# Closing stretch of a fused attention and expert-FFN kernel: gathered rows added before the last shared sum, a chained gather queue, and a re-cut last product

## The chip, the cores and the metric

One NeuronCore of a Trainium2 chip. The metric is the device time of one execution in microseconds; before the change the median of three runs is 760.45 (760.0 to 761.2).

## The reference, cut to what matters

```python
x = x + xattn(layernorm(x), ctx, ctx, Wq, Wk, Wv, Wfc, bfc)      # 8 x 256 tokens of 512 numbers
h = layernorm(x)                                                  # 2048 tokens in all
scores = softmax(h @ gate.T)                                      # 8 experts in 4 groups of 2
topk_w, topk_i = top 2 experts of the 2 best groups
routed = sum over the 2 experts of topk_w * ((silu(h @ gate_w.T) * (h @ up_w.T)) @ down_w.T)
shared = (silu(h @ sh_gate_w.T) * (h @ sh_up_w.T)) @ sh_down_w.T  # 704 wide: two halves of 352
x = x + routed + shared                                           # float32 out
```

## The kernel before, in words

Everything runs on one core. Attention takes the first 290 us, the output projection, second layernorm and routing run to about 390 us. The feed-forward part works in units: one unit is a tile of 128 tokens times one set of gate, up and down weights, and has a number w. `PA` = 16 units are the two halves of the shared expert on the first 8 token tiles ("early" tiles 0 to 7). `PB` = 36 units (slots) are the routed experts on tokens that were collected by expert; each writes its 128 result rows to `slot_y` in DRAM. `PC` = 16 units are the two halves of the shared expert on the last 8 token tiles ("late" tiles m = 0 to 7, token tile m + 8); their numbers run from `C0` to `TOTAL` - 1. The change is in this last part and a step ahead of it.

Weights and activations are cut in two float16 parts, so each product is made of three. A unit w goes like this. TensorE makes the gate product and then the up product (`gate_up`, L1510: 24 matmuls of 352 columns). ScalarE makes the silu (L1133). VectorE multiplies it with the up product (`hidden`, L2015); ScalarE squares and sums (L1138), VectorE turns the sum into a scale (L2020, L2023), ScalarE writes the scaled high part in float16 (L1143), VectorE the low part (`hidden_low`, L2028), which counts `h_cut`. SyncE then issues a DMA that transposes the hidden rows into `hT` (`h_rows`, L637). TensorE makes the down product from it (`down`, L1527: 9 matmuls of 512 columns) into bank 4 or 5. VectorE adds this product, scaled, to a row buffer (`add_down`, L2042), which counts `y_evac`. The scale comes from `down_factor` (L2036).

TensorE's order is up(w), down(w-2), up(w+1), down(w-1), and so on, so the down product of a unit comes two units after its up product. At the end there is no more up product: down(TOTAL-3), down(TOTAL-2), then six transposes on TensorE (L1690) in place of the DMA for the last unit, copies of both parts out of PSUM (high part ScalarE L1208, low part VectorE L2507), and the last down product (L1697).

The result of a token tile is x2 (the residual, loaded by SyncE into `res_out[q]`, L698) plus the shared sums plus two gathered rows of `slot_y`, each times a weight. `gather_1[q]` and `gather_2[q]` are filled by two indirect DMAs that GpSimd issues (L943); q = 2m is early tile m, q = 2m + 1 is late tile m. Every q has buffers of its own, and four semaphores (q % 4) count the gathers, four the residual loads. From q = 4 on GpSimd waits before the gathers of q until the output of q - 4 is finished (`out_done`). For a late tile VectorE adds the two shared products to `res_out` (`late_sum`), then, half a tile later, the two gathered rows (`late_out`, L2449 and L2452, the second one written to `gather_2[q]`). For an early tile, whose shared part is in x2 already, it only adds the gathered rows (`early_out`, L2428 and L2432). SyncE stores `gather_2[q]` (L702, the last tile L769). The last late tile adds its gathered rows first (L2512, L2514), and then both shared products.

All engines run an order written out by hand, and each engine issues strictly in that order. In the loop of VectorE (L2485) a round of m does unit (m, 0), then `late_out(m-2)` and `late_sum(m-1, 0)`, then unit (m, 1), an early output, and `late_sum(m-1, 1)`. On SyncE an `h_rows(w)`, a store that waits for its output, and loads follow each other in one queue.

`load_late` loads the transposed tokens of a late tile (L691). The first two of these loads are issued when SyncE comes to w = C0 - 2.

Of the kernel before, what the change touches and what calls it, by code (L numbers as in the profile page):

```python
# [30 lines left out]
P = 128  # L31
# [53 lines left out]
def build(nc, x, ctxT, wqT, wkvT, wfcT, bfc, gwT, wgu, wdn, out):  # L85
# [17 lines left out]
    with ExitStack() as ctx:  # L103
# [309 lines left out]
        TOTAL = PA + PB + PC  # L413
        LAST_PAR = (TOTAL - 1) % 2

        def early_done(m):
            return 2 * m if m < 3 else 2 * m - 1

        def late_done(m):
            return 2 * m + 1 if m < 2 else 2 * m + 2  # L420
# [9 lines left out]
        def _(sp):  # L430
# [269 lines left out]
            def store_out(t, done, q):  # L700
                sp.wait_ge(out_done, done + 1)
                sp.dma_start(tile_of(out_tiles, t), gather_2[q]).then_inc(out_st[q % 4], 16)  # L702
# [11 lines left out]
            for w in range(B0, C0):  # L714
# [19 lines left out]
                if m == SLOTS + 1:  # L734
                    for s in range(2):
                        sp.wait_ge(sx_ld[s], SX_SEEN + 16 * len(range(FIRST_ROWS + s, SLOTS, 2)))
                        load_late(s, s)

            def store_pair(m, side):
                store_out(m + side * EARLY, late_done(m) if side else early_done(m), 2 * m + side)  # L740

            for w in range(C0, TOTAL):
# [3 lines left out]
                if c == 0 and m >= 2:  # L746
                    store_pair(m - 2, 1)
                    if m < EARLY - 1:
                        load_pair(m, 1)
# [3 lines left out]
                if c == 1 and 1 <= m < EARLY - 1:  # L753
                    side_m = m - 1 if m < 3 else m
                    store_pair(side_m, 0)
                    load_pair(side_m + 2, 0)
                if c == 0 and m == EARLY - 1:
                    load_pair(m, 1)
                if c == 0 and m == 3:
                    store_pair(2, 0)  # L760
                    load_pair(4, 0)
# [4 lines left out]
            store_pair(EARLY - 1, 0)  # L766
            store_pair(EARLY - 2, 1)
# [7 lines left out]
        def _(pool):  # L775
# [160 lines left out]
            for q in range(2 * EARLY):  # L936
                t, m = q // 2 + q % 2 * EARLY, q // 2 - 2
                if q >= 4:
                    pool.wait_ge(out_done, (late_done(m) if q % 2 else early_done(m)) + 1)
# [272 lines left out]
        def _(pe):  # L1212
# [473 lines left out]
            late_down(TILES - EARLY - 1, 0)  # L1686
            pe.wait_ge(h_cut, TOTAL)
            for a in range(2):
                for j in range(NF):
                    tr = nc.tensor.transpose(last_hT[a][:, j, :], h16[LAST_PAR][:, a, j * P:(j + 1) * P], ident16)  # L1690
            tr.then_inc(xt_ready, 1)
            pe.wait_ge(h_high, TOTAL + 1)
            pe.wait_ge(h_cut, TOTAL + 1)
            pe.wait_ge(y_evac, TOTAL - 2)
            for j in range(NF):
                for n, (hp, wp) in enumerate(((0, 0), (0, 1), (1, 0))):
                    mm = nc.tensor.matmul(bank[Y_BANKS[LAST_PAR]][:], hT[LAST_PAR][:, hp, j, :], shared_dn(1)(wp, j),  # L1697
                                          start=(j == 0 and n == 0), stop=(j == NF - 1 and n == 2))
            mm.then_inc(dn_done, 1)
# [3 lines left out]
        def _(dve):  # L1703
# [718 lines left out]
            def early_out(m, half):  # L2422
# [4 lines left out]
                if half != 1:  # L2427
                    nc.vector.scalar_tensor_tensor(res_out[q], gather_1[q], w1[:, m:m + 1], res_out[q],  # L2428
                                                   ALU.mult, ALU.add).then_inc(step, 1)
                if half != 0:  # L2430
                    dve.wait_ge(step, links4 + early_done(m) + 1)
                    nc.vector.scalar_tensor_tensor(gather_2[q], gather_2[q], w2[:, m:m + 1], res_out[q],  # L2432
                                                   ALU.mult, ALU.add).then_inc(out_done, 1)

            def late_sum(m, c):
# [137 lines left out]
```

## Time and profile before

| what | value |
|---|---|
| median of 3 runs | 760.45 us |
| the profiled execution | 761.22 us |
| its span in the profile | 759.3 us |
| TensorE busy (matmul) | 734.4 us, 97% of the span |
| VectorE / ScalarE / GpSimd busy | 561.4 / 418.1 / 265.1 us |
| granted TensorE clock, mean | 0.993 of full |

The span is one execution as the hardware profiler saw it; the execution's own time has 1.9 us around it. "Busy" of TensorE counts each matmul from its issue to its modelled end, and they overlap. A row of a timeline gives the start in us, the duration, the engine, the line of the kernel, the operation and its tiles. In brackets stands how long the engine was idle before and what ended that. SPq is SyncE's queue: its rows are issues of DMAs, not the transfers.

### The profile page before, as it was taken

What the parts mean: (1) busy time and instruction counts of PE and PEld (TensorE: products, weight loads), DVE (VectorE), ACT (ScalarE), POOL (GpSimd) and SP (SyncE); (2) the same over time, 40 slices, a digit from 0 to 9 for tenths busy, and PEclk for the clock granted to TensorE, in tenths of its full rate; (3) what the DMA queues carried; (4) which work ended last, traced back from release to release, by engine and by line L of the source; (5) the groups of instructions that cost most, each with busy time, mean ns of one, the idle gap of its engine ahead of it and who ended that gap; (6) DMA issues with size and microseconds to landing.
All of it is one profiled execution on the core that took longest, in us unless ns stands there. A gap on an engine that the chain in (4) does not pass through costs nothing.

```text
span 759.3 us, 16085 instructions
## 1 busy us (share of the span) xinstructions
PE 734.4 (97%) x5316; PEld 398.3 (52%) x5317; DVE 561.4 (74%) x1191; ACT 418.1 (55%) x845; POOL 265.1 (35%) x219
## 2 busy tenths in 40 slices
PE   6999999999999999999999899999999999999997
PEld 4554534443344335666655456555555556655553
DVE  5677779999999967897589787555555555447767
ACT  3567568888888884777632554343434334232232
POOL 3254007999996302556200021111111110015431
PEclk9999989999999999999999999999999999999999
DMA  8998846565664798997586564977777789549995
GB/s 326 353 413 259 252 151 207 180 197 165 201 182 131 238 370 324 358 398 239 170 230 195 147 155 123 190 180 180 183 170 184 172 180 206 139 116 297 278 263 158
DMA packets 155099, 168.15 MB, mean 221 GB/s; under 512 B 97952, under 2 KB 111776, under 8 KB 154528
## 3 DMA queue, kind: packets, MB, share of 16 engines
q1 hardware_dynamic: 143724, 126.20, 57.1%
q0 software_dynamic: 10720, 40.12, 17.4%
q10 hardware_dynamic: 596, 1.07, 0.4%
q8 instruction: 35, 0.57, 0.3%
q14 instruction: 24, 0.20, 0.1%
HBM read 104.09 MB, written 41.42 MB: 192 GB/s over the span
## 4 chain that ended last, share of the span: by engine, by line
PE 78%; DVE 10%; ACT 4%; DMA 4%; issue 3%; SPq 1%; DVEq 0%; ACTq 0%
PE psum L1510 24%; PE psum L1527 13%; PE psum L1356 9%; PE psum L1342 6%; PE psum L1437 6%; PE psum L1270 4%; PE psum L1512 3%; PE psum L1246 3%; PE psum L1373 2%; PE psum L1529 2%; PE psum L1455 1%; PE psum L1222 1%; DMA x_dram<-sb_rows 1%; DVE sb_stats L1742 1%; ACT sb_weights L1064 1%
## 5 line engine op out<-in xcount | busy, mean ns | idle before, releaser
L1510 PE MATMUL psum<-sb_weights,sb_rows 128*128 128x352 f16 (+1 forms) x1344 | 209.7, 313 | 0.9 <-DVE sb_h L2028 0.6
L1510 PEld LDWEIGHTS psum<-sb_weights,sb_rows 128*128 128x128 f16 x1344 | 131.2, 98 | 77.7 <-issue 1.9
L1761 DVE TENSOR_REDUCE sb_rows<-psum 128x4 f32<-128x1024 f32 x128 | 149.9, 1214 | 4.5 <-PE psum L1270 4.5
L1064 ACT ACTIVATE sb_weights<-psum 128x512 f32<-128x512 f32 x256 | 139.4, 595 | 23.1 <-PE psum L1342 19.9
L1527 PE MATMUL psum<-sb_weights,sb_hT 128*128 128x512 f16 (+1 forms) x531 | 125.4, 382 | 0.0
L923 POOL DMA_INDIRECT sb_rows<-xn_rows,sb_slot_tok x36 | 35.5, 986 | 209.3 <-DVE sb_rows L2394 134.6
L1138 ACT ACTIVATE psum<-psum 128x352 f32<-128x352 f32 x68 | 30.5, 448 | 118.4 <-DVE psum L2015 118.3
L1342 PE MATMUL psum<-sb_weights 50*128 50x512 f16 x256 | 87.2, 390 | 1.7 <-ACT sb_weights L1064 0.9
L1356 PE MATMUL psum<-sb_weights 128*32 128x256 f32 x1024 | 83.1, 397 | 0.3
L1527 PEld LDWEIGHTS psum<-sb_weights,sb_hT 128*128 128x128 f16 x531 | 51.9, 98 | 56.0 <-issue 2.2
L1270 PE MATMUL psum<-sb_weights 48*128 48x256 f16 x512 | 71.3, 275 | 0.6 <-DVE sb_rows L1761 0.4
L943 POOL DMA_INDIRECT sb_weights<-slot_y,sb_p_i x32 | 31.7, 990 | 81.2 <-DMA slot_y<-sb_rows 42.6
L1437 PE MATMUL psum<-sb_weights 128*128 128x512 f32 x128 | 58.2, 597 | 0.3 <-ACT sb_weights L1070 0.3
L2028 DVE SCALAR_TENSOR_TENSOR sb_h<-psum,sb_h_scale_i,sb_h 128x352 f16<-128x352 f32 x68 | 39.6, 583 | 22.5 <-ACT sb_h L1143 22.4
L2015 DVE SCALAR_TENSOR_TENSOR psum<-psum,sb_inv_now,sb_h 128x352 f32<-128x352 f32 x36 | 21.3, 593 | 45.6 <-PE psum L1510 33.6
L1342 PEld LDWEIGHTS psum<-sb_weights 50*128 50x128 f16 x256 | 23.5, 93 | 55.1 <-ACT sb_weights L1064 45.9
L1133 ACT ACTIVATE sb_h<-psum,sb_inv_now 128x352 f32<-128x352 f32 x36 | 19.9, 553 | 50.6 <-PE psum L1510 38.5
L1246 PE MATMUL psum<-sb_weights 128*128 128x512 f16 x192 | 44.9, 380 | 2.5 <-DVE sb_weights L1811 1.3
L1143 ACT ACTIVATE sb_h<-psum,sb_h_scale_i 128x352 f16<-128x352 f32 x68 | 37.6, 553 | 17.2 <-DVE sb_h_scale_i L2020 17.2
L829 POOL TENSOR_TENSOR sb_weights<-sb_weights,sb_w_scale_i 128x1408 f32<-128x1408 f32 x15 | 38.0, 2531 | 23.3 <-ACT sb_weights L1110 22.5
L839 POOL TENSOR_TENSOR sb_weights<-sb_weights 128x1408 f16<-128x1408 f32 x15 | 43.0, 2863 | 1.2
L1133 ACT ACTIVATE sb_h<-psum,sb_w_inv_i 128x352 f32<-128x352 f32 x32 | 17.7, 554 | 45.8 <-PE psum L1510 44.9
(304 smaller groups left out, 1161.0 us busy)
## 6 DMA issues: line engine op xcount, KB each, us to landing
sb_weights<-in_wgu SPq DMA_DIRECT2D x20, 704.0 KB, 7.1
sb_weights<-in_wgu POOLq DMA_DIRECT2D x20, 704.0 KB, 6.0
sb_weights<-in_wdn SPq DMA_DIRECT2D x17, 768.0 KB, 5.7
slot_y<-sb_rows SPq DMA_DIRECT2D x36, 256.0 KB, 2.3
sb_weights<-q_parts SPq DMA_DIRECT2D x96, 64.0 KB, 2.9
x_dram<-sb_rows SPq DMA_DIRECT2D x24, 256.0 KB, 4.4
q_parts<-sb_weights SPq DMA_DIRECT2D x16, 256.0 KB, 4.1
sb_rows<-in_x POOLq DMA_DIRECT2D x16, 256.0 KB, 5.2
```

Of the source, the lines that this page charges most:

```text
L829: nc.gpsimd.tensor_tensor(stage, stage, scale.broadcast_to([P, HALF]), ALU.mult).then_inc(gu_scaled, 1)
L839: nc.gpsimd.tensor_tensor(low, stage, high, ALU.subtract).then_inc(gu_cut, 1)
L1064: nc.scalar.activation(probs[G % 2][:, kt, pair * 512:(pair + 1) * 512], bank[4 + f % 2], ACT.Exp, scale=exp_by[n]).then_inc(exp_done, 1)
L1246: mm = nc.tensor.matmul(bank[Q_BANKS[n][m]], wq16[:, wp, k, m * P:(m + 1) * P], xnT[n % 2][:, xp, k, :], start=(k == 0 and i == 0), stop=( ...
L1270: mm = nc.tensor.matmul(bank[banks[qt] + side][:, h * SEQ:(h + 1) * SEQ], q_st[s][lo:hi, g, h, b * SEQ + qt * P:b * SEQ + (qt + 1) * P], k ...
L1342: nc.tensor.matmul(bank[4 + side].rearrange("p (h t) -> p h t", h=HH), k_st[s][lo:hi, g, b * SEQ + kt * P:b * SEQ + (kt + 1) * P], q_st[s] ...
L1356: mm = nc.tensor.matmul(bank[6][VW * c:VW * (c + 1), 0:SEQ], v_now, probs[G % 2][:, kt, c * SEQ:(c + 1) * SEQ], start=(kt == 0), stop=(kt ...
L1437: mm = nc.tensor.matmul(bank[2 + s][:], oT[s][:, k, :], wfc_sb[:, k, :], start=(k == 0), stop=(k == KD - 1))
L1510: mm = nc.tensor.matmul(to[:, 0:F], x_T[:, at:at + P], gu(wp, k, which), start=first, stop=last)
L1527: mm = nc.tensor.matmul(bank[Y_BANKS[par]][:], hT[par][:, hp, j, :], dn(wp, j), start=first, stop=last)
L1761: nc.vector.tensor_reduce(to[:, :, j // UB, :, j % UB, qt], psum[:, banks[qt] * 512:(banks[qt] + 2) * 512] .rearrange("p (a h k) -> p a h ...
L2028: nc.vector.scalar_tensor_tensor(h16[par][:, 1, 0:F], bank[GU_BANKS[par][1]][:, 0:F], h_scale[:, par:par + 1], h16[par][:, 0, 0:F], ALU.mu ...
```

## The change

Parts, in the order of the diff:

- The first two `load_late` are issued at w = C0 - 3 instead of C0 - 2 (`m == SLOTS`), behind the same wait for the transposes of the routed slots' rows.
- The early outputs have other places: `EARLY_AT` says after which unit of the late part each is added and stored, the last two (6 and 7) both in unit (6, 0).
- Late tiles 0 and 1 are as before. From m = 2 on the gathered rows are added between the two shared sums (`late_gathered`, in unit (m+1, 1)), and the second shared sum goes to `gather_2[q]` and finishes the output. Late tile 6 and 7 have an order of their own at the end. SyncE stores these late tiles by `y_evac` instead of `out_done`.
- GpSimd's gathers of q >= 4 wait for the gathers of q - 4 to land, no longer for an output.
- On TensorE the six last transposes stand after the fifth of the nine matmuls of down(TOTAL-2). The last down product is made in two halves of 256 columns, into banks 0 and 1, 18 matmuls in all, with a count after each half; VectorE adds it in two halves as well.

```diff
         TOTAL = PA + PB + PC
+        last_y = [bank[b] for b in GU_BANKS[TOTAL % 2]]
         LAST_PAR = (TOTAL - 1) % 2
 
+        SUM_FIRST = 2
+        EARLY_AT = {(1, 1): (0,), (2, 1): (1,), (3, 0): (2,), (4, 0): (3, 4), (5, 0): (5,), (6, 0): (6, 7)}
+
         def early_done(m):
-            return 2 * m if m < 3 else 2 * m - 1
+            return min(2 * m, m + SUM_FIRST)
 
         def late_done(m):
-            return 2 * m + 1 if m < 2 else 2 * m + 2
+            return 2 * m + 1
+
+        def late_summed(m):
+            return C0 + 2 * m + 2
 
         def shared_inv(c):
...
-                if m == SLOTS + 1:
+                if m == SLOTS:
                     for s in range(2):
                         sp.wait_ge(sx_ld[s], SX_SEEN + 16 * len(range(FIRST_ROWS + s, SLOTS, 2)))
                         load_late(s, s)
...
-            def store_pair(m, side):
-                store_out(m + side * EARLY, late_done(m) if side else early_done(m), 2 * m + side)
+            def store_early(m):
+                sp.wait_ge(out_done, early_done(m) + 1)
+                store_out(m, 2 * m)
+
+            def store_late(m):
+                if m < SUM_FIRST:
+                    sp.wait_ge(out_done, late_done(m) + 1)
+                else:
+                    sp.wait_ge(y_evac, late_summed(m))
+                store_out(m + EARLY, 2 * m + 1)
...
-                if c == 0 and m >= 2:
-                    store_pair(m - 2, 1)
-                    if m < EARLY - 1:
-                        load_pair(m, 1)
+                if c == 0 and 2 <= m < 2 + SUM_FIRST:
+                    store_late(m - 2)
+                    load_pair(m, 1)
...
-                if c == 1 and 1 <= m < EARLY - 1:
-                    side_m = m - 1 if m < 3 else m
-                    store_pair(side_m, 0)
-                    load_pair(side_m + 2, 0)
-                if c == 0 and m == EARLY - 1:
-                    load_pair(m, 1)
-                if c == 0 and m == 3:
-                    store_pair(2, 0)
-                    load_pair(4, 0)
+                for e in EARLY_AT.get((m, c), ()):
+                    store_early(e)
+                    load_pair(e + 2, 0)
+                if c == 1 and SUM_FIRST < m < EARLY - 1:
+                    store_late(m - 1)
+                    load_pair(m + 1, 1)
...
-            store_pair(EARLY - 1, 0)
-            store_pair(EARLY - 2, 1)
+            store_late(EARLY - 2)
...
-                t, m = q // 2 + q % 2 * EARLY, q // 2 - 2
+                t = q // 2 + q % 2 * EARLY
                 if q >= 4:
-                    pool.wait_ge(out_done, (late_done(m) if q % 2 else early_done(m)) + 1)
+                    pool.wait_ge(gat_ld[q % 4], q // 4 * 32)
...
-            late_down(TILES - EARLY - 1, 0)
-            pe.wait_ge(h_cut, TOTAL)
-            for a in range(2):
-                for j in range(NF):
-                    tr = nc.tensor.transpose(last_hT[a][:, j, :], h16[LAST_PAR][:, a, j * P:(j + 1) * P], ident16)
-            tr.then_inc(xt_ready, 1)
+            def last_transposes():
+                pe.wait_ge(h_cut, TOTAL)
+                for a in range(2):
+                    for j in range(NF):
+                        tr = nc.tensor.transpose(last_hT[a][:, j, :], h16[LAST_PAR][:, a, j * P:(j + 1) * P], ident16)
+                tr.then_inc(xt_ready, 1)
+
+            m, par = TILES - EARLY - 1, (TOTAL - 2) % 2
+            pe.wait_ge(hT_ld[par], (m + C0 // 2) * 16 + 16)
+            pe.wait_ge(y_evac, TOTAL - 3)
+            for j in range(NF):
+                for n, (hp, wp) in enumerate(((0, 0), (0, 1), (1, 0))):
+                    mm = nc.tensor.matmul(bank[Y_BANKS[par]][:], hT[par][:, hp, j, :], shared_dn(0)(wp, j),
+                                          start=(j == 0 and n == 0), stop=(j == NF - 1 and n == 2))
+                    if (j, n) == (1, 1):
+                        last_transposes()
+            mm.then_inc(dn_done, 1)
             pe.wait_ge(h_high, TOTAL + 1)
             pe.wait_ge(h_cut, TOTAL + 1)
-            pe.wait_ge(y_evac, TOTAL - 2)
-            for j in range(NF):
-                for n, (hp, wp) in enumerate(((0, 0), (0, 1), (1, 0))):
-                    mm = nc.tensor.matmul(bank[Y_BANKS[LAST_PAR]][:], hT[LAST_PAR][:, hp, j, :], shared_dn(1)(wp, j),
-                                          start=(j == 0 and n == 0), stop=(j == NF - 1 and n == 2))
-            mm.then_inc(dn_done, 1)
+            for half in range(2):
+                here = slice(half * D // 2, (half + 1) * D // 2)
+                for j in range(NF):
+                    for n, (hp, wp) in enumerate(((0, 0), (0, 1), (1, 0))):
+                        mm = nc.tensor.matmul(last_y[half][:, 0:D // 2], hT[LAST_PAR][:, hp, j, :], shared_dn(1)(wp, j)[:, here],
+                                              start=(j == 0 and n == 0), stop=(j == NF - 1 and n == 2))
+                mm.then_inc(dn_done, 1)
...
+            def late_sum(m, c, to=None):
 
                 q, n = 2 * m + 1, m // 2
                 if c == 0:
                     dve.wait_ge(cx2_ld[q % 4], n * 16 + (16 + CX2_SEEN))
                 else:
                     dve.wait_ge(y_evac, m * 2 + (C0 + 1))
-                add_down(m * 2 + (C0 + c), (C0 + c) % 2, (C0 + c) % 2, res_out[q])
+                if to is not None:
+                    dve.wait_ge(step, steps[0])
+                add_down(m * 2 + (C0 + c), (C0 + c) % 2, (C0 + c) % 2, res_out[q] if to is None else to)
+
+            def late_gathered(m, half, summed):
+
+                q, n, t = 2 * m + 1, m // 2, m + EARLY
+                if half != 1:
+                    if summed:
+                        dve.wait_ge(y_evac, m * 2 + (C0 + 1))
+                    dve.wait_ge(cx2_ld[q % 4], n * 16 + (16 + CX2_SEEN))
+                    dve.wait_ge(gat_ld[q % 4], n * 32 + 32)
+                    nc.vector.scalar_tensor_tensor(res_out[q], gather_1[q], w1[:, t:t + 1], res_out[q],
+                                                   ALU.mult, ALU.add).then_inc(step, 1)
+                    steps[0] += 1
+                if half != 0:
+                    dve.wait_ge(step, steps[0])
+                    nc.vector.scalar_tensor_tensor(gather_2[q], gather_2[q], w2[:, t:t + 1], res_out[q],
+                                                   ALU.mult, ALU.add).then_inc(step, 1)
+                    steps[0] += 1
...
-            for m in range(2, EARLY):
+            for m in range(2, last):
                 late_unit(m, 0)
                 late_low(m, 0)
-                late_out(m - 2)
+                if m < 2 + SUM_FIRST:
+                    late_out(m - 2)
                 late_sum(m - 1, 0)
                 late_factor(m, 0)
-                if m == 3:
-                    early_out(2, None)
-                if m == last:
-                    early_out(last, 0)
-                    hidden(m * 2 + (C0 + 1), (C0 + 1) % 2, shared_inv(1))
-                    early_out(last, 1)
-                    hidden_factor(m * 2 + (C0 + 1), (C0 + 1) % 2)
-                    late_low(m, 1)
+                for e in EARLY_AT.get((m, 0), ()):
+                    early_out(e)
+                late_unit(m, 1)
+                late_low(m, 1)
+                if m > SUM_FIRST:
+                    late_gathered(m - 1, None, True)
+                    late_sum(m - 1, 1, gather_2[2 * m - 1])
                 else:
-                    late_unit(m, 1)
-                    late_low(m, 1)
-                    early_out(m - 1 if m < 3 else m, None)
-                late_sum(m - 1, 1)
+                    for e in EARLY_AT.get((m, 1), ()):
+                        early_out(e)
+                    late_sum(m - 1, 1)
                 late_factor(m, 1)
-            late_out(last - 1)
+            m, to, q = last, gather_2[2 * last - 1], TILES - 1
+            late_unit(m, 0)
+            late_low(m, 0)
+            late_gathered(m - 1, None, False)
+            late_sum(m - 1, 0, to)
+            late_factor(m, 0)
+            hidden(m * 2 + (C0 + 1), (C0 + 1) % 2, shared_inv(1))
+            late_gathered(m, 0, False)
+            hidden_factor(m * 2 + (C0 + 1), (C0 + 1) % 2)
+            late_low(m, 1)
+            late_sum(m - 1, 1, to)
             dve.wait_ge(xt_ready, SLOTS + 1)
             nc.vector.tensor_copy(hT[LAST_PAR][:, 1, :, :], last_hT[1]).then_inc(h_cut, 1)
-            m, q = last, TILES - 1
-            dve.wait_ge(cx2_ld[q % 4], m // 2 * 16 + (16 + CX2_SEEN))
-            dve.wait_ge(gat_ld[q % 4], m // 2 * 32 + 32)
-            link = chain(links4 + late_done(m - 1) + 1)
-            link(nc.vector.scalar_tensor_tensor(res_out[q], gather_1[q], w1[:, TILES - 1:TILES], res_out[q],
-                                                ALU.mult, ALU.add))
-            link(nc.vector.scalar_tensor_tensor(gather_2[q], gather_2[q], w2[:, TILES - 1:TILES], res_out[q],
-                                                ALU.mult, ALU.add))
-            for c in range(2):
-                if c == 1:
-                    dve.wait_ge(y_evac, TOTAL - 1)
-                add_down(TOTAL - 2 + c, (C0 + c) % 2, (C0 + c) % 2, gather_2[q])
+            late_factor(m, 1)
+            late_gathered(m, 1, False)
+            late_sum(m, 0, gather_2[q])
+            par = (C0 + 1) % 2
+            dve.wait_ge(y_evac, TOTAL - 1)
+            dve.wait_ge(y_factor, TOTAL)
+            for half in range(2):
+                here = slice(half * D // 2, (half + 1) * D // 2)
+                dve.wait_ge(dn_done, TOTAL + half)
+                done = nc.vector.scalar_tensor_tensor(gather_2[q][:, here], last_y[half][:, 0:D // 2], y_scale[:, par:par + 1],
+                                                      gather_2[q][:, here], ALU.mult, ALU.add)
+            done.then_inc(y_evac, 1)
```

## Rows read from the trace of the kernel before

**Rows 1.** The page: busy time, and the group of the gathers.

```profile
PE 734.4 (97%) x5316; PEld 398.3 (52%) x5317; DVE 561.4 (74%) x1191; ACT 418.1 (55%) x845; POOL 265.1 (35%) x219
...
L943 POOL DMA_INDIRECT sb_weights<-slot_y,sb_p_i x32 | 31.7, 990 | 81.2 <-DMA slot_y<-sb_rows 42.6
```

**Rows 2.** Waits, 655 to 760 us: who waited for whom, total, times, longest.

```profile
PE psum L1697 <- ACT sb_hT L1208: 1.6, 1, 1.6
...
PE psum L1510 <- DMA sb_rows<-xnT_dram: 0.3, 1, 0.3
```

**Rows 3.** Timeline of TensorE where the first two late units begin.

```profile
660.27 0.38 PE L1531 MATMUL psum<-sb_weights,sb_hT 128*64 128x512 f16 x1
660.96 3.75 PE L1510 MATMUL psum<-sb_weights,sb_rows 128*128 128x352 f16 x24 [0.31 <-DMA sb_rows<-xnT_dram]
...
666.40 0.38 PE L1531 MATMUL psum<-sb_weights,sb_hT 128*64 128x512 f16 x1
666.71 3.75 PE L1510 MATMUL psum<-sb_weights,sb_rows 128*128 128x352 f16 x24
```

**Rows 4.** Timeline of SyncE's queue ahead of that.

```profile
647.75 2.09 SPq L708 DMA_TRANSPOSE sb_rows<-sb_rows  x1
...
658.26 0.92 SPq L691 DMA_DIRECT2D sb_rows<-xnT_dram  x2
```

**Rows 5.** Timeline of VectorE: units (3,0), (3,1), (4,0) and a factor.

```profile
698.34 0.59 DVE L2015 SCALAR_TENSOR_TENSOR psum<-psum,sb_w_inv_i,sb_h 128x352 f32<-128x352 f32 x1 [0.52 <-PE psum L1510]
...
704.71 0.59 DVE L2015 SCALAR_TENSOR_TENSOR psum<-psum,sb_w_inv_i,sb_h 128x352 f32<-128x352 f32 x1
...
709.62 0.58 DVE L2015 SCALAR_TENSOR_TENSOR psum<-psum,sb_w_inv_i,sb_h 128x352 f32<-128x352 f32 x1
...
714.40 0.21 DVE L2036 TENSOR_SCALAR sb_stats<-sb_h_root,sb_dn_inv_i 128x1 f32<-128x1 f32 x1
```

**Rows 6.** Chain that ended last, 733 to 757 us: start, length, what.

```profile
733.38 3.58 PE psum L1510 x24
736.96 1.94 PE psum L1527 x9
...
756.00 0.75 DVE sb_weights L2042
```

**Rows 7.** Timeline of all engines, 744 us to the end.

```profile
744.26 3.74 PE L1510 MATMUL psum<-sb_weights,sb_rows 128*128 128x352 f16 x24
...
747.78 0.75 DVE L2428 SCALAR_TENSOR_TENSOR sb_weights<-sb_weights,sb_w 128x512 f32<-128x512 f32 x1 [0.25 <-issue]
747.84 4.05 PE L1527 MATMUL psum<-sb_weights,sb_hT 128*128 128x512 f16 x18
...
748.45 0.58 DVE L2015 SCALAR_TENSOR_TENSOR psum<-psum,sb_w_inv_i,sb_h 128x352 f32<-128x352 f32 x1
...
750.42 0.58 DVE L2028 SCALAR_TENSOR_TENSOR sb_h<-psum,sb_h_scale_i,sb_h 128x352 f16<-128x352 f32 x1 [0.42 <-ACT sb_h L1143]
...
751.73 0.50 PE L1690 MATMUL psum<-sb_tri,sb_h 128*128 128x128 f16 x6
...
752.32 0.48 ACT L1208 COPY sb_hT<-psum 128x384 f16<-128x384 f16 x1 [1.93 <-PE psum L1690]
...
753.35 0.35 DVE L2507 COPY sb_hT<-psum 128x384 f16<-128x384 f16 x1
...
753.80 2.10 PE L1697 MATMUL psum<-sb_weights,sb_hT 128*128 128x512 f16 x9 [1.58 <-ACT sb_hT L1208]
...
756.78 0.33 SPq L769 DMA_DIRECT2D out<-sb_weights  x1
```

**Rows 8.** Transposing DMAs of the hidden rows, 680 to 760 us: issue to landing.

```profile
DMA to landing us min/median/max: 2.7/3.9/6.6
```

**Rows 9.** Stretches: length; busy PE, PEld, DVE, ACT, POOL; clock; DMA share; GB/s.

```profile
680.00:700.00 20.00, 20.00 (x120) 11.58 (x119) 12.26 (x27) 6.33 (x16) 13.02 (x14) 1.00 0.99 271
700.00:720.00 20.00, 20.00 (x124) 11.91 (x122) 15.45 (x31) 5.83 (x14) 7.92 (x8) 1.00 1.00 305
```

More of the change, by code:

```diff
@@ L698, in load_res, with store_out @@
                 sp.dma_start(res_out[q], tile_of(x2_dram, t)).then_inc(cx2_ld[q % 4], 16)
-            def store_out(t, done, q):
-                sp.wait_ge(out_done, done + 1)
+            def store_out(t, q):
                 sp.dma_start(tile_of(out_tiles, t), gather_2[q]).then_inc(out_st[q % 4], 16)
@@ L2419, in _, with early_out @@
                 slot_factor(m, m % 2)
-            def early_out(m, half):
+            def early_out(m):
                 q, n = 2 * m, m // 2
@@ L2426, in early_out @@
                 dve.wait_ge(gat_ld[q % 4], n * 32 + 32)
[L2427 to L2435, printed above, removed]
+                nc.vector.scalar_tensor_tensor(res_out[q], gather_1[q], w1[:, m:m + 1], res_out[q],
+                                               ALU.mult, ALU.add).then_inc(step, 1)
+                steps[0] += 1
+                dve.wait_ge(step, steps[0])
+                nc.vector.scalar_tensor_tensor(gather_2[q], gather_2[q], w2[:, m:m + 1], res_out[q],
+                                               ALU.mult, ALU.add).then_inc(out_done, 1)
+            def late_sum(m, c, to=None):
                 q, n = 2 * m + 1, m // 2
@@ L2441, in late_sum @@
                     dve.wait_ge(y_evac, m * 2 + (C0 + 1))
-                add_down(m * 2 + (C0 + c), (C0 + c) % 2, (C0 + c) % 2, res_out[q])
+                if to is not None:
[12 more added lines that the diff above has]
+                if half != 0:
+                    dve.wait_ge(step, steps[0])
+                    nc.vector.scalar_tensor_tensor(gather_2[q], gather_2[q], w2[:, t:t + 1], res_out[q],
+                                                   ALU.mult, ALU.add).then_inc(step, 1)
+                    steps[0] += 1
             def late_out(m):
@@ L2450, in late_out @@
                                                ALU.mult, ALU.add).then_inc(step, 1)
-                dve.wait_ge(step, links4 + late_done(m) + 1)
+                steps[0] += 1
+                dve.wait_ge(step, steps[0])
                 nc.vector.scalar_tensor_tensor(gather_2[q], gather_2[q], w2[:, t:t + 1], res_out[q],
@@ L2480, in _ @@
             late_low(1, 1)
-            early_out(0, None)
+            early_out(0)
             late_sum(0, 1)
```

2 lines of the change are left out of this document (1 added, 1 removed).

## The prediction

> **What bounds the kernel now.** I read the page's busy times first: TensorE is busy 97% of the span, the next engine, VectorE, 74% [rows 1]. So the question is when TensorE is *not* running in the stretch that is changed, and that is what the table of waits answers: between 655 and 760 us TensorE waited twice, 0.3 us for a load at the start of the late part and 1.6 us for the copy of the transposed rows before the very last product [rows 2]. In between it works through a fixed grid: an up product of 3.58 us (24 matmuls) and a down product of 1.94 us (9 matmuls), 5.52 us per unit [rows 6]. Nothing that VectorE, GpSimd or SyncE do faster between 662 and 748 us can move that grid. Only three places can: the load's wait, the chain from the last up product to the last down product, and what follows the last down product. I then read the timeline around each [rows 3, 4, 7].
>
> **Part 1, the first late loads one step earlier.** The last down matmul of a slot starts at 660.27 and the up product at 660.96, 0.69 later; the same change-over six us later takes 0.31 (666.40 to 666.71) [rows 3]. The difference, about 0.37 us, is the wait. The loads were issued at 658.26 [rows 4]. One step earlier in SyncE's order they come behind the last transposing DMA of the slots, issued at 647.75 and 2.09 long, whose landing they wait for. Transposes of hidden rows land 2.7 to 6.6 us after issue [rows 8], so I take 650.5 to 654.4 for it; two issues take 0.92, so the loads are out by 655.3 at the latest, 3 us sooner than now and 5 us before they are needed. What is moved past in SyncE's queue is the `h_rows` of the next unit, which comes one 5.52 us unit after the one before it and is not due until then. Gain 0.37; bounds 0 (the load still lands last) and 0.37.
>
> **Part 2, the order of outputs and sums, and the chained gathers.** The number of 512-column VectorE operations stays the same. What is new: in units (4,0) and (6,0) VectorE has a sum and four output operations in a row, and a second shared sum waits for the gathered add just ahead of it. Such a full unit stands in the trace: from the start of unit (3,0)'s `hidden` to that of (3,1) 6.37 us pass (698.34 to 704.71), 0.85 over the grid; from (3,1) to (4,0), with two output operations and a sum, 4.91 us (to 709.62), so 0.61 is made up per unit [rows 5]. From (6,0) the backlog is 0.85 at (6,1). With 0.12 for the lost overlap of the dependent sum (an estimate: 0.08 by which VectorE's operations overlap, 748.53 against 748.45 [rows 7], and a semaphore of 0.03 to 0.04 as in 756.75 to 756.78 [rows 6, 7]) it is 0.36 at (7,0) and below zero at (7,1). Cost 0, hidden by the grid; were the cover gone, 0.36 us would reach the end. A late `hidden` does not touch TensorE before: `h_cut` of unit w is 2.55 us after its `hidden` (1.97 + 0.58 [rows 7]), and the up product that needs it starts 7.46 us after the last one ended.
>
> The gathers: from first to last they now spread over 31.7 us of issue and 81.2 - 42.6 = 38.6 us of idle [rows 1]. Without the wait for outputs some part of the 38.6 goes, so the last ones land up to 38 us earlier, long before the outputs that use them. Nobody in the waits stood still for a gather [rows 2], so this gains 0. Its cost is traffic: from 680 to 700 us, with 13 us of gather issue, the DMA engines are 0.99 busy, from 700 to 720 us already 1.00 with only 8 [rows 9]. The slack that pays for it: a transpose issued 2.6 us after its up product is needed 11.04 us after it, so 8.4 us from issue, and the longest took 6.6 [rows 8]. Cost 0; bounds 0 and the rival below.
>
> **Part 3, the closing chain.** The last up product ends at 748.00 (744.26 + 3.74), but `hidden` starts at 748.45, because an early output sits ahead of it (747.78 + 0.75 = 748.53) [rows 7]. After the change that place is empty: the gathered add of the last tile stands behind `hidden`. So `hidden` starts at 748.04, 0.41 earlier, and `hidden_low`, 1.97 later, runs from 750.01 to 750.59.
>
> The 18 down matmuls from 747.84 are 0.216 apart [rows 6, 7]; the second product begins at 749.78 and its fifth matmul's place ends at 750.86. That is where the transposes now start (the rows are ready at 750.59 plus 0.1), against 751.73. ScalarE's copy begins 0.59 after the transposes begin (752.32) and takes 0.48: 751.45 to 751.93. VectorE's copy, 0.35, waited for by two output operations before (753.35), now has only a 0.75 sum ahead of it, done at 751.3: 751.45 to 751.80. TensorE follows a copy by 0.10 (753.70 to 753.80) [rows 7], which gives 752.03; its own queue has six transposes (0.33 to 0.50) and four matmuls (0.86) from 750.86, so 752.05 to 752.22. I take 752.1 for the start of the last product, against 753.80: 1.7 us.
>
> The halves: 3.58 / 24 = 0.149 us for 352 columns and 1.94 / 9 = 0.216 for 512 make 0.415 ns per column and 0.109 for 256 [rows 6]. 18 of them take 1.97 us, as 9 whole ones did. The last one ends 0.16 after its place (2.10 - 1.94 [rows 6, 7]): 754.23. A VectorE operation of this kind takes 0.58 for 352 and 0.75 for 512 columns, so 0.48 for 256. VectorE itself is ready for the second half at about 754.1: copy to 751.80, factor 0.21 [rows 5], gathered add 0.75, sum 0.75, first half 0.48 and some 0.04 between each. So the end of the last add is 754.27 + 0.48 = 754.75, against 756.00 + 0.75 = 756.75 [rows 6]. The store and its landing stay as they are. Gain 2.00. Bounds: 1.6 if TensorE starts at 752.22 and the halves save nothing (754.35 + 0.04 + 0.75 = 755.14), 2.2 if the copies and the transposes overlap a little more.
>
> Two rules of the Trainium skill are weighed against this part. "TensorE: Matmul & The Clock Gate", Back-to-back issue gap, gives 262 cycles for 256 columns and 518 for 512, and a separate sustained figure of 131 ns for 512. The trace has 216 ns for 512, so by the trace the cycle figures hold here and the sustained one doesn't; by them two halves cost 6 cycles more than a whole product, 0.02 us over nine pairs. "VectorE: DVE Perf Modes", the section on the TRN2 errata, says an operation pays a fixed cost and that tiles should have 512 elements or more, which speaks against the two half adds. The rows agree that there is one, about 0.2 us. It is paid twice, but the first time lies under the second half of the product. The page's figure for a PSUM source (120 cycles and one per element at 0.96 GHz, 0.39 us for 256) would make the sum 0.09 larger.
>
> **Sum.** 0.37 + 0 + 2.00 = 2.37 us. Against the profiled execution's 761.22 that is 758.85; the profiled one is 0.77 above the median, so on the median of 760.45 it is 758.1. Its own range is 757.4 to 758.8.
>
> **Rivals.**
> 1. *The transpose of unit TOTAL-2 lands late.* This one has no 8.4 us: with the 0.36 of backlog it is issued at about 745.5 and needed at 749.7, 4.2 us later. It landed in 2.7 with nothing beside it; now a store and a load go out just ahead of it, about 742.7. Against: gathers no longer run there. At 5.9 us the stall is 1.7: 759.8; at the longest landing, 6.6, it is 2.4 and the gain is gone: 760.5.
> 2. *VectorE sets the end.* If the backlog of the double outputs isn't made up and `hidden` comes 0.85 late instead of on time, all of part 3 moves by it: 758.1 + 0.85 = 758.95. For: VectorE has only 0.1 to spare before the second half. Against: the 0.61 per unit.
> 3. *The first loads do not come sooner in effect* (the change does not do what it says): 0.37 less, 758.5. For: they wait for transposes in a busy stretch.
> 4. *Slower: the dense gathers hold up the transposes between 690 and 720 us.* Eight more gathers of 256 KB in the 20 us from 700 add 105 GB/s to 305, where the engines are full [rows 9]. From a landing of 8.4 us down products wait. A stall delays the next three units together, so six units make two stalls; slower than before from 9.6 us, and at 10.4 us it is 2 x 2.0 - 2.37 = +1.6: 762.1. Against: 6.6 was the longest with 13 gathers in a stretch, and the gathers limit themselves by waiting for those of q - 4.
>
> **Chances.** Forecast 0.60, rival 1 0.12, rival 2 0.12, rival 3 0.08, rival 4 0.06, others 0.02. A measurement of this kernel can tell about 0.2%, 1.5 us, from no change; faster means under 758.9. The forecast gives 0.56 of that, rival 2 half of its share, rival 3 most: 0.69. Slower is rival 4: 0.06. The range 757.4 to 760.2 leaves out rival 4, the worse end of rival 1 and a little below.
>
> **What would show it.** TensorE's waits: no load at 660 us and none of 1.6 us before the last product. The last up product ends at about 747.6 and `hidden` follows within 0.1. Transposes begin 2.9 us after that end, the last product 4.1, the final store 6.8 (now 8.8). If a wait for `hT` stands before down(TOTAL-2), rival 1; waits before down products around 700 to 720 us, rival 4; `hidden` over 0.3 behind the last up product, rival 2. The prediction is wrong in kind if the up product ends later than 748.0.

## The result, and the profile after

The changed kernel took 782.66 us (median of 4, 782.05 to 785.86), the kernel before beside it 760.83 (760.0 to 764.17): a ratio of 1.0287, 95% interval 1.0245 to 1.0329. It is slower by 22 us, where 758.1 was forecast, outside the range. The profiled execution has a span of 780.4 us against 759.3.

The first view is again the page: busy times, the clock row, and the group of the gathers.

```profile
PE 740.1 (95%) x5325; PEld 399.2 (51%) x5326; DVE 561.5 (72%) x1192; ACT 418.4 (54%) x845; POOL 264.8 (34%) x219
...
PEclk9999999999999999999999999999999999995899
...
L952 POOL DMA_INDIRECT sb_weights<-slot_y,sb_p_i x32 | 31.3, 979 | 53.2 <-DMA slot_y<-sb_rows 42.0
```

Beside [rows 1] the idle time of the gathers went from 81.2 to 53.2 us, as meant, and the clock row has one slice at 5, about 702 to 722 us, and one at 8 after it. That slice is where to look. The stretches of the changed kernel (length; busy PE, PEld, DVE, ACT, POOL; granted clock; DMA share; GB/s):

```profile
680.00:700.00 20.00, 20.00 (x122) 11.75 (x120) 11.66 (x26) 4.98 (x12) 13.93 (x15) 1.00 0.95 256
700.00:720.00 20.00, 8.14 (x28) 2.54 (x26) 2.87 (x6) 1.66 (x4) 15.12 (x17) 0.63 0.84 265
720.00:740.00 20.00, 16.40 (x78) 8.01 (x78) 11.42 (x24) 3.88 (x9) 1.80 (x2) 0.77 0.62 178
740.00:760.00 20.00, 20.00 (x124) 11.93 (x122) 14.94 (x33) 6.64 (x16) 0.00 (x0) 1.00 0.68 184
```

Against [rows 9], 700 to 720 us has 28 matmuls instead of 124, and VectorE and ScalarE do as little; only GpSimd works on, 17 gathers instead of 8. Over these 20 us the DMA engines are *less* busy than before, 0.84 instead of 1.00 (full only at the start, 1.09 from 700 to 704 us). The whole loss lies here: 96 matmuls missing in this stretch and 42 in the next (78 instead of 120) are 23 us of a grid that has 33 in 5.52 us. The mean granted clock of the stretch is 0.63, so most of it runs at the lower level, 1.2 GHz. The clock is still at 1.00 from 700 to 704 us, where TensorE has begun to idle, so it fell after the idling and did not cause it. It is at 1.00 again from 730 us.

What ended TensorE's idle time stands in its timeline (start, length, what, and in brackets the idle time before it):

```profile
698.81 2.11 PE L1536 MATMUL psum<-sb_weights,sb_hT 128*128 128x512 f16 x9
700.75 0.76 PE L1519 MATMUL psum<-sb_weights,sb_rows 128*128 128x352 f16 x4
701.90 0.46 PE L1519 MATMUL psum<-sb_weights,sb_rows 128*128 128x352 f16 x2 [0.38 <-issue]
702.61 0.31 PE L1519 MATMUL psum<-sb_weights,sb_rows 128*128 128x352 f16 x1 [0.25 <-issue]
703.32 0.61 PE L1519 MATMUL psum<-sb_weights,sb_rows 128*128 128x352 f16 x3 [0.40 <-issue]
705.44 0.74 PE L1519 MATMUL psum<-sb_weights,sb_rows 128*128 128x352 f16 x2 [1.52 <-issue]
...
724.39 4.15 PE L1536 MATMUL psum<-sb_weights,sb_hT 128*128 128x512 f16 x8 [0.82 <-issue]
```

The rows from 700.75 to 705.44 are *inside* one up product, whose 24 matmuls wait for nothing between them. "issue" is idle time for which the trace shows no wait. The starts 701.90, 702.61, 703.32 are 0.71 apart, and 705.44 three times that: instructions reach TensorE one or a few at a time. The last row shows what the clock adds: eight down matmuls take 4.15 us at the lower level (0.50 from 724 to 728 us), where nine take 2.11 at the upper. The other engines, from the product before to the end of the stall:

```profile
695.23 3.74 PE L1519 MATMUL psum<-sb_weights,sb_rows 128*128 128x352 f16 x24
...
704.14 0.55 ACT L1142 ACTIVATE sb_h<-psum,sb_w_inv_i 128x352 f32<-128x352 f32 x1 [8.05 <-remote]
...
716.02 0.59 DVE L2036 SCALAR_TENSOR_TENSOR psum<-psum,sb_w_inv_i,sb_h 128x352 f32<-128x352 f32 x1 [16.89 <-remote]
...
718.01 0.58 DVE L2049 SCALAR_TENSOR_TENSOR sb_h<-psum,sb_h_scale_i,sb_h 128x352 f16<-128x352 f32 x1 [0.42 <-issue]
...
721.16 0.95 POOL L952 DMA_INDIRECT sb_weights<-slot_y,sb_p_i  x1 [0.30 <-issue]
...
725.89 1.21 SPq L644 DMA_TRANSPOSE sb_hT<-sb_h  x1
```

The up product ended at 698.97, and ScalarE's silu of it starts 5.2 us later. VectorE's `hidden` needs that silu, done at 704.69, and starts 11.3 us later. SyncE's queue needs the rows that VectorE has finished at 718.59, and issues their transpose 7.3 us later. What runs has its usual length (0.55, 0.59). So these are not engines waiting for each other: four instruction streams hardly move, though what they need is there, while GpSimd issues a gather each 1.25 us. They do not recover together. VectorE and ScalarE run a whole chain in their usual rhythm from 716.02 to 720.03 us, with gathers still going out; TensorE and SyncE's queue come back after the last gather, issued at 721.16.

The rest of the prediction can be read beside it. No load is waited for at 660 us, and the end of the changed kernel is this:

```profile
767.35 3.74 PE L1519 MATMUL psum<-sb_weights,sb_rows 128*128 128x352 f16 x24
...
771.41 0.58 DVE L2036 SCALAR_TENSOR_TENSOR psum<-psum,sb_w_inv_i,sb_h 128x352 f32<-128x352 f32 x1
...
774.03 0.51 PE L1699 MATMUL psum<-sb_tri,sb_h 128*128 128x128 f16 x6
...
775.24 2.13 PE L1718 MATMUL psum<-sb_weights,sb_hT 128*128 128x256 f16 x18
...
776.59 0.48 DVE L2566 SCALAR_TENSOR_TENSOR sb_weights<-psum,sb_stats,sb_weights 128x256 f32<-128x256 f32 x1
777.41 0.48 DVE L2566 SCALAR_TENSOR_TENSOR sb_weights<-psum,sb_stats,sb_weights 128x256 f32<-128x256 f32 x1 [0.33 <-PE psum L1718]
777.92 0.33 SPq L778 DMA_DIRECT2D out<-sb_weights  x1
```

From the end of the last up product (771.09) the transposes begin 2.94 us later, the last product 4.15, the store 6.83; it was 8.78 [rows 7].

### The profile page after: what moved, and what is told of

It reads as the page before. It is cut to its first block, busy times and chain, and to the rows that moved or that the text cites. A ratio compares the mean times of both kernels' runs of the same rounds, so it can differ in the third digit from the quotient of the medians.

```text
span 780.4 us, 16110 instructions
## 1 busy us (share of the span) xinstructions
PE 740.1 (95%) x5325; PEld 399.2 (51%) x5326; DVE 561.5 (72%) x1192; ACT 418.4 (54%) x845; POOL 264.8 (34%) x219
## 4 chain that ended last, share of the span: by engine, by line
PE 79%; DVE 7%; DMA 6%; issue 4%; ACT 3%; SPq 2%; DVEq 0%; ACTq 0%
PE psum L1519 24%; PE psum L1536 13%; PE psum L1365 7%; PE psum L1446 7%; PE psum L1351 5%; PE psum L1521 4%; PE psum L1255 4%; PE psum L1279 3%; DMA sb_weights<-k_parts 3%; PE psum L1538 2%; PE psum L1382 2%; PE psum L1231 2%; DMA sb_weights<-in_x 1%; PE psum L1464 1%; PE psum L1236 1%
## 5 line engine op out<-in xcount | busy, mean ns | idle before, releaser
L1519 PE MATMUL psum<-sb_weights,sb_rows 128*128 128x352 f16 (+1 forms) x1344 | 214.1, 314 | 13.3 <-issue 12.8
L952 POOL DMA_INDIRECT sb_weights<-slot_y,sb_p_i x32 | 31.3, 979 | 53.2 <-DMA slot_y<-sb_rows 42.0
```

The source lines that it names most:

```text
L1519: mm = nc.tensor.matmul(to[:, 0:F], x_T[:, at:at + P], gu(wp, k, which), start=first, stop=last)
```

## The experiments

The theory after the result: gathers that follow each other without a gap keep the other engines from issuing. In all experiments but the first every transposing transfer is a plain copy of the same bytes; "plain" means that below. Each group that ran together shares its runs of the kernel before; ratios are to these, and between groups only ratios are compared.

**A small program.** Are such gathers enough by themselves? Each stage gives every engine a fixed load and GpSimd one of eight tasks.

```
for q in range(pairs):                       # 16 pairs of 2 gathers
    if q >= back: pool.wait_ge(gat[(q - back) % 4], done[q - back])
```

> A small program of its own that leaves the whole computation out and writes zeros. In each of eight stages TensorE has 192 matmuls 128x512 f16 (41 us at 0.216), ScalarE 64 copies 128x512, VectorE 48 sums 128x512 and SP's queue 12 loads of 0.26 MB (36 in the last two), while GpSimd has in turn: nothing; 16 pairs of gathers, each waiting for the pair four earlier to land; the same with a 0.95 us fill after each pair; 32 plain loads in place of the gathers; two pairs under way instead of four; only 6 pairs; nothing beside 36 loads; 16 pairs beside 36 loads. Theory (gathers without a gap starve the issue of the other engines by themselves): stages 2, 5 and 8 are 15 to 25 us longer than stage 1, stages 3 and 6 within 3 us of it. Rival M (the stall needs what else is queued in the kernel, loads, stores and transposes): stage 2 within 2 us of stage 1, and only stage 8 longer, if any. Rival D (it is the depth under way): stage 5 as stage 1. Rival G (it is the indirect addressing): stage 4 as stage 1; if it is the software queue as such, stage 4 as stage 2.

It took 406.5 us. Its stretches, first in the stage without gathers, then with 16 pairs, then with 16 pairs beside 36 loads:

```profile
30.00:40.00 10.00, 10.00 (x48) 4.51 (x46) 10.00 (x17) 10.00 (x20) 0.00 (x0) 1.00 0.39 107
...
80.00:90.00 10.00, 10.00 (x49) 4.52 (x47) 9.20 (x15) 10.00 (x21) 7.56 (x9) 1.00 0.93 312
...
370.00:380.00 10.00, 10.00 (x48) 4.51 (x46) 10.00 (x17) 10.00 (x20) 7.56 (x9) 1.00 1.04 387
```

TensorE has 48 matmuls in 10 us in all of them, also beside gathers in the rhythm of the stall (7.56 us of GpSimd in 10, as there) with the DMA engines at 1.04. The stages with 16 pairs came out longer only because the gathers themselves run on after the other work (in stage 3, with the fills, to 164.13 us, where TensorE has finished at 149.17). The first form of the theory, gathers by themselves, did not hold on this chip. The program has no loops, though, and TensorE and ScalarE run loops in the late part of the kernel.

**The plain kernels.** Does the stall need the transposing transfers?

```
-                sp.dma_start(hT[s]..., h_sb[s]..., transpose=True)
+                sp.dma_start(hT[s]..., h_sb[s]...)
```

> The kernel before with every transposing transfer (of the hidden rows and of the gathered slot rows) as a plain copy of the same bytes; so the rows stand untransposed in the down products, and this part of the computation is changed, here and in the runs called plain. It is the base for them. The copies should land sooner than the 2.7 to 6.6 us of the transposes, the order of the work stays: 752 to 762 us, no stall between 700 and 725 us.

> The changed kernel with plain copies. Theory L (the gathers without a gap starve the other engines where these run loops and much else is queued, whatever it is): the stall of 700.9 to 725 us is there again, 19 to 24 us over the plain before. Theory T (the stall needs transposing transfers in the same stretch, since the small program had none and no stall): no stall, 1.5 to 2.5 us under the plain before.

Plain before: 759.5 us (10 runs, 756.8 to 761.6), ratio to the kernel before 0.9970 (0.9955 to 0.9986). Plain changed: 782.15 (4 runs, 781.5 to 782.9), ratio 1.0268 (1.0250 to 1.0286). The stall is there without a single transposing transfer; rival T fell. One expectation was missed on the way: the copies do not land sooner, 4.7 us in the middle (2.1 to 5.6, in q1 below) against 3.9 for the transposes (2.7 to 6.6).

**Parts put back or taken alone.** These four ran together, on a second chip, without the plain changed kernel beside them. So a run without a stall says little here until it is known that the chip shows one.

> The changed kernel with plain copies, and one thing put back: each of the 12 late pairs of gathers waits again until the output four pairs earlier is summed. Theory L (gathers without a gap, in this kernel): the stall goes, what the first loads (0.38) and the closing chain (1.95) gave stays: 756.5 to 758 us against 759.5 of the plain before. Rival A (the new order of outputs and sums on VectorE and of stores and loads in SP's queue made the stall): within 3 us of the 782.2 of the plain changed kernel.

> The kernel before with plain copies and one thing of the change: the late pairs of gathers wait only for the pair four earlier to have landed. Theory L: the whole loss by itself, 759.5 + 19 to 24 us = 779 to 784 us. Rival A (orders): 759 to 761 us.

> The plain changed kernel with one fill 128x1024 on GpSimd (0.97 us) after each of the 12 late pairs; the waits stay those of the change. If pace decides, the stall is gone or under 8 us: 757 to 765 us. If it needs only that gathers are never waited for: still over 775 us.

> The plain changed kernel with each of the 32 gathers as an ordinary load of 128 rows of the same table through the same software queue, same bytes and same waits (the summed rows are then others). If the stall comes of the indirect addressing: gone, 757 to 759 us. If of many transfers of the software queue under way: still there, 770 to 783 us. GpSimd issues such a load in 0.55 us instead of 0.98, so the rate is higher.

The edits: in o3 the gathers wait for `out_done` and `y_evac` of four pairs earlier; o4 is the plain before with `pool.wait_ge(gat_ld[q % 4], q // 4 * 32)` alone; o5 is the plain changed kernel with

```
+                if q >= 4:
+                    pool.wait_ge(pause, q - 4)
+                    nc.gpsimd.memset(rows[:, 4 * D:6 * D], 0.0).then_inc(pause, 1)
```

and o6 has `nc.gpsimd.dma_start(to, slot_y_tiles[2 * q + n])` for each gather. None stalled:

| run | us, median (range), runs | ratio, 95% interval |
|---|---|---|
| o3 old waits | 761.6 (757.8 to 764.8), 10 | 1.0023 (1.0001 to 1.0044) |
| o4 before, chained | 758.7 (757.4 to 760.6), 10 | 0.9974 (0.9951 to 0.9996) |
| o5 fill after each pair | 755.4 (754.4 to 758.2), 7 | 0.9939 (0.9911 to 0.9968) |
| o6 plain loads | 758.5 (756.0 to 764.3), 10 | 0.9966 (0.9938 to 0.9993) |

o4 is a miss for the theory: the same chained gathers in the kernel before, and no loss. o3 went half as expected, no stall but none of the gain. Its waits say why (engine, line, releaser: total, times, longest):

```profile
DVE sb_weights L2455 <- DMA sb_weights<-slot_y,sb_p_i: 3.8, 1, 3.8
...
PE psum L1714 <- DVE sb_weights L2070: 1.8, 1, 1.8
PE psum L1706 <- DVE sb_h L2056: 1.5, 1, 1.5
```

VectorE stands 3.8 us for a gather and hands the delay on to TensorE at the end. The new order of outputs takes its rows earlier, so it *needs* gathers that run ahead of the outputs; it can't be had with the old pacing. (The other way round it can: o4 has the gathers without the new order.) In o6 TensorE lost some 2.5 us for another reason, a down product that waited 2.3 us for its rows while the loads, 0.55 us each to issue, filled the DMA engines at 1.04: the shape of rival 4, in small.

**The same program on other chips.** Before reading more into these, the control was repeated beside three more variants, on a third chip.

> The plain changed kernel once more, beside the three runs that follow on the same chip. If the stall belongs to the program: 781 to 784 us. If it belongs to the chip that ran it first: 755 to 759 us.

> The plain changed kernel with one single fill 128x1024 (0.97 us) on GpSimd, after the seventh pair of gathers, ahead of where the stall began; all later gathers follow without a gap. If the stall needs a state that has built up by then over the unbroken row of gathers: it begins later or not at all, 755 to 770 us. If it is the row of gathers after it that counts: 778 to 783 us.

> The plain changed kernel with each late pair of gathers waiting for the pair two earlier to have landed instead of four earlier. If a gather lands 5 us after its issue (its row here when nothing stalls), two pairs under way pace GpSimd to 4 gathers in some 7 us instead of 5: no stall, 755 to 760 us. If the depth plays no part and the rhythm stays 1.25 us: 778 to 783 us.

> The plain changed kernel with the first loads of the late tiles one step later again, as before. If the stall belongs to the chained gathers with the new order of outputs: still 781 to 784 us. If the earlier loads take part in it: 756 to 760 us.

The edits are `if q == 6:` on one fill; `gat_ld[(q - 2) % 4]` in the gathers' wait; and `if m == SLOTS + 1:` on the first late loads. The control did not stall: 756.0 us (754.0 to 758.6, 8 runs), ratio 0.9942 (0.9919 to 0.9966). One fill 756.3 (0.9945), two pairs 757.1 (0.9946), late loads 755.9 (0.9935). With a control like that the three say nothing of the stall, and the forecasts that they met say nothing either. The pair that does was run last, again on the second chip:

> The plain changed kernel a third time, control of the run that follows on the same chip. Either 781 to 784 us in all executions or 754 to 759 us in all; if both appear on one chip, it is a matter of the execution and not of the chip.

> The plain changed kernel with a fill of 0.97 us on GpSimd after each of the 12 late pairs of gathers. If the control stalls: 754 to 758 us if the pace of the gathers brings the stall, over 775 us if it does not. If the control does not stall: 754 to 758 us, and the fill costs nothing.

Control: 782.9 us (780.4 to 785.2, all 4), ratio 1.0281 (1.0236 to 1.0326). With the fill: 756.6 (753.6 to 759.6, all 7), ratio 0.9929 (0.9900 to 0.9959). This is the cleanest comparison of the study, though the executions of one program in one session all agree and so count as one trial each. The stretches of three kernels, first the plain changed one that stalled (s1):

```profile
690.00:700.00 10.00, 7.56 (x41) 3.71 (x38) 3.87 (x8) 1.11 (x3) 7.56 (x9) 0.95 0.86 283
700.00:710.00 10.00, 2.92 (x7) 0.73 (x7) 0.00 (x0) 0.00 (x0) 7.56 (x9) 0.50 0.89 308
710.00:720.00 10.00, 2.26 (x5) 0.41 (x4) 0.00 (x0) 0.55 (x1) 5.45 (x6) 0.50 0.64 190
```

then the same program on the chip where it did not (q1):

```profile
700.00:710.00 10.00, 10.00 (x61) 5.77 (x60) 7.47 (x17) 3.10 (x8) 7.56 (x9) 1.00 1.02 373
710.00:720.00 10.00, 10.00 (x61) 5.77 (x60) 7.54 (x16) 2.99 (x8) 6.17 (x7) 1.00 1.04 395
```

and with the fill (s2), where GpSimd's busy time contains the fills:

```profile
700.00:710.00 10.00, 10.00 (x63) 5.99 (x62) 8.06 (x16) 2.77 (x6) 8.60 (x9) 1.00 0.97 332
710.00:720.00 10.00, 10.00 (x62) 5.92 (x61) 7.63 (x17) 3.33 (x8) 8.60 (x10) 1.00 0.97 307
```

s1 and q1 have the same nine gathers from 700 to 710 us. In q1 the DMA engines are fuller (1.02 against 0.89), and in s1 they are at 0.74 from 696 to 698 us, where its stall begins. So full DMA engines are not what stalls the others. Nor is an unbroken row of gathers enough on that chip: q1 has nine of them 1.25 us apart from 705.60 to 715.63 us, and TensorE loses nothing.

**Where the stall begins and ends.** The three traces with a stall (the changed kernel, o2, s1) agree on both. ScalarE is late first: its silu of unit (3, 0) begins 2.07 us after the start of that unit's products in q1, so it was due at 697.3, 694.8 and 693.4 us, and came at 704.1, 708.0 and 718.7. TensorE goes on at its full rate for 2.6 to 3.9 us more. Its first gap of over 0.6 us between two starts is at 701.2, 698.2 and 696.0 us, each time with 16 of the 32 gathers out, and within four matmuls of the start of the products of unit (3, 1). The gathers keep step with TensorE's program up to there, so which of the two marks counts can't be told. The last packet of the gathers' queue ends at 724.4, 720.5 and 719.6 us, and TensorE's last such gap ends 1.4, 2.1 and 1.8 us later. So in all three TensorE's stall lasts until the gathers have landed, and not much longer.

## Why the prediction was wrong

- **Part 1 was right.** The wait at 660 us is gone. From the `hidden` of the last slot but one to the next it takes 5.62 us instead of 6.00, so 0.38 gained for 0.37 forecast, and rival 3 is out. In total time it can't be seen: q4, without it, is at 0.9935 against 0.9942.
- **Part 3 was right.** The store comes 6.83 us after the last up product instead of 8.78, so 1.95 gained for 2.00 forecast; in two plain kernels that do not stall it is 6.74 (q1) against 8.77 (o1). The half adds took 0.48 each, as the rows had it. In q1 the backlog of the double outputs is near what part 2 made it: `hidden` comes 0.88, 0.45 and 0.04 us after the product at (6, 1), (7, 0) and (7, 1), for 0.85, 0.36 and none forecast. It is made up by 0.43 per unit and not 0.61, which just suffices. So rival 2 did not come by itself. It came with the stall, which leaves VectorE behind: `hidden` is 0.32 late at the end of the changed kernel, where it cost under 0.1, but 0.85 in s1 and 2.04 in o2, where the store comes 7.36 and 8.55 after the last up product, and most of this gain is lost in o2. No wait for rows stands before down(TOTAL-2), so rival 1 did not come.
- **The sum fits where the stall is absent**: 0.9942 (q1) against 0.9970 (o1) is 0.28%, 2.1 us of 760, for 2.37 forecast; the two intervals make it about 0 to 4 us. These are plain kernels on two chips. No run shows the changed kernel itself, with its transposes, free of the stall.
- **The step that failed is part 2, "Cost 0; bounds 0 and the rival below" for the chained gathers.** In the plain kernels it measured 0 on one chip and 25 to 26 us on two others (1.0268 and 1.0281 against 0.9942, of 760.9 us). The rival, that the dense gathers hold up the transposes, had the right place and the right culprit, but its price came from the landing of transposes, and no row after it shows TensorE waiting for one there. Its argument was about bytes: the DMA engines at 1.00 and eight gathers more. The runs show the opposite picture, engines at 0.84 and streams that are not issued. The argument about slack (8.4 us against 6.6) was sound and of no use, since it asked only what waits for a transfer, and not what GpSimd's unbroken issue does to the other queues.
- **Part 2's other half**, the order of outputs and sums, costs nothing, but not by itself: with the old pacing of the gathers (o3) the order of outputs is 0.8% slower than with the fill (1.0023 against 0.9939, same chip, side by side).

How far the cause is shown. What fails is shown: the instruction streams of TensorE, ScalarE, VectorE and SyncE nearly stand still for some 20 to 25 us. That the gathers bring it is supported from two sides: s1 stalled and s2, with pauses between the gathers, did not, in one session on one chip; and in three traces TensorE's stall ends just after the last gathers have landed. But the trials are few. Chained gathers with the new order stalled in three sessions (the result, o2, s1) and did not in one (q1), and the version with a fill after each pair was free in both of its sessions, o5 and s2, on one chip. A program that stalls in most sessions but not in all could have been lucky twice. So that the pause cures is likely and not proven.

That the gathers alone suffice is not shown: the small program (on a chip that may not be one that shows the stall) and o4 had none, and o4 ran on the chip where the plain changed kernel stalled later. So another part of the change may join in; which one was not found. The late loads, one fill and two pairs under way were tried only where the control didn't stall either. Whether the difference between the chips is one of the chip, or of how the program was loaded there, is open: within a session all executions agreed (4, 4, 8 and 4).

Nor is the mechanism settled. One candidate is the fetch of instructions. The Trainium skill, "Runtime: NRT & Kernel Launch", Instruction fetch mechanics, says that each sequencer fetches its next block through a DMA queue of its own, and that a taken branch out of its window must wait for such a fetch. TensorE and ScalarE do run loops here. But the traces speak against it. No instruction packet stands between 700 and 740 us in any of them, of stalled or free runs. In the changed kernel the next ones after 695 us come at 767.95 and 776.42 us, long after the stall, so no late fetch ended it. And the whole execution has as many as one that is free. The pages of the changed kernel and of q1 (packets, MB, share of 16 engines):

```profile
q8 instruction: 36, 0.59, 0.3%
q14 instruction: 24, 0.20, 0.1%
...
q8 instruction: 35, 0.57, 0.3%
q14 instruction: 24, 0.20, 0.1%
```

(The 36th of q1 comes at 755.01 us, after the span of 753.8.) VectorE and SyncE's queue have no loop in this part and stand still as well. What is in flight in s1 from 696 to 720 us is this:

```profile
q0 software_dynamic: 1491, 4.86, 65.2%
q1 hardware_dynamic: 576, 0.98, 11.3%
```

So the stall has another mechanism than fetches of code, as far as these queues show them all, and which one it is stays open.

**A version that beats both.** The plain changed kernel with one fill after each late pair is at 0.9939 and 0.9929 in two sessions, on a chip that shows the stall, where the plain before had 0.9970 on another chip and, beside o5 on the same one, o4 had 0.9974: 2 to 3 us below them. No cost of the fills is seen; GpSimd has no other work there. That the same edit does it with the transposing transfers was not tried.

## What to carry to other kernels

A wait that paces an engine off the critical path may be what leaves room for the others: before it is taken away, ask what the engine does when it never pauses, and try a pause of its own in its place (here 0.97 us after each pair of gathers). When several engines idle at once with "issue" or "remote" before them and the DMA engines are not full, look for the one engine that does not idle. And repeat the control beside each group of variants: three variants here looked like cures until the control, on that chip, was well too. When all executions of one loaded program agree, more of them do not make the case stronger; another session or chip does.

## What the hardware showed that was not expected

- In the stall instructions reach TensorE on a grid of 0.71 us (701.90, 702.61, 703.32, 705.44), while each runs as long as its clock has it (0.31 for 352 columns at 1.00, 0.45 at 0.50); ScalarE, VectorE and SyncE's queue stand for 5.2, 11.3 and 7.3 us with their inputs ready.
- The same program had medians of 782.2 and 782.9 us on two chips (780.4 to 785.2, 8 executions) and of 756.0 on a third (754.0 to 758.6, also 8). Four agreeing runs on one chip say nothing of another.
- In three traces TensorE's stall began with 16 of the 32 gathers issued, 2.6 to 3.9 us after ScalarE's next silu had been due, and ended 1.4 to 2.1 us after the last packet of the gathers.
- Gathers are issued each 1.25 us (0.95 and a gap of 0.30) and move 201 to 213 GB/s when they are alone (stretches of 4 us from 708 to 720); plain loads in their place go out in 0.55 us and fill the DMA engines to 1.04.
- A fill of 128x1024 on GpSimd takes 0.97 us and hides wholly beside 62 matmuls in 10 us.
